# Choosing two experts of eight on GpSimd instead of VectorE in a fused attention and mixture-of-experts kernel

## The reference

```python
h = _layernorm(x) * (1 + ca) + sa
x = x + ga * attn(h)          # 16 heads of width 8, softmax, a norm over the whole sample
h = _layernorm(x) * (1 + cb) + sb
logits = h @ gate_w                                   # [token, 8]
top_vals, top_idx = jax.lax.top_k(logits, 2)          # of equals, the lower index first
gate_scores = softmax(top_vals)
x = x + gb * sum_k gate_scores[k] * expert[top_idx[k]](h)
```

## Time and profile before

| | |
|---|---|
| time, median of 3 runs | 1099.64 us (1099.56 to 1099.70) |
| profiled execution, whole | 1099.41 us |
| its span | 1097.5 us |
| mean granted PE clock over the span | 0.972 |
| busy: PE, DVE, ACT, POOL | 947.5, 922.9, 796.9, 664.2 us |
| the 1024 maxima (L1234) | 643.0 us, 680 ns each |
| the 1024 exponentials (L1773) | 544.3 us, 603 ns each |

### The profile page before, as it was taken

The page is one execution under the profiler, slowest core; times in us unless marked ns, Lnnn a source line. Parts: engine busy times, 40 slices in busy tenths (PEclk is TensorE's granted clock), DMA queues, the critical chain, the costliest instruction groups (busy, mean ns, idle before and its releaser), DMA issues. The chain is left out here.

```text
span 1097.5 us, 19321 instructions
## 1 busy us (share of the span) xinstructions
PE 947.5 (86%) x5725; PEld 360.7 (33%) x5725; DVE 922.9 (84%) x2045; ACT 796.9 (73%) x1493; POOL 664.2 (61%) x1033
## 2 busy tenths in 40 slices
PE   4699888998999999899998999888798999699970
PEld 2122222222222222222222222222125766466640
DVE  5788989999999999999999999999765677255666
ACT  2128888888888888888888888888676687477640
POOL 4843132675856768566685665634637667777772
PEclk9999999999999999999999999999879999899995
DMA  8979766856667566775656757522332454454556
GB/s 214 140 144 243 154 183 131 152 154 106 162 138 141 160 115 171 135 146 146 129 166 122 156 141 136 151 77 67 86 100 76 154 167 138 132 158 129 185 169 244
DMA packets 369047, 159.61 MB, mean 145 GB/s; under 512 B 290656, under 2 KB 333552, under 8 KB 365232
## 3 DMA queue, kind: packets, MB, share of 16 engines
q1 hardware_dynamic: 347376, 122.06, 50.3%
q10 hardware_dynamic: 12480, 17.57, 5.0%
q0 software_dynamic: 9088, 18.76, 4.9%
HBM read 87.85 MB, written 71.82 MB: 145 GB/s over the span
## 5 line engine op out<-in xcount | busy, mean ns | idle before, releaser
L1234 DVE TENSOR_REDUCE neg_max<-bank 128x1 f32<-128x512 f32 x1024 | 643.0, 680 | 34.6 <-PE bank L1998 31.8
L1773 ACT ACTIVATE probs<-bank 128x512 f32<-128x512 f32 x1024 | 544.3, 603 | 94.8 <-PE bank L2010 91.9
L1998 PE MATMUL bank<-Kt,Qt 48*128 48x512 bf16 x1024 | 339.1, 396 | 61.7 <-DVE neg_max L1234 47.3
L2010 PE MATMUL bank<-Qt,Kt 51*128 51x512 bf16 x1024 | 329.9, 390 | 6.2 <-ACT probs L1773 5.9
L2023 PE MATMUL bank<-probs,Vt 128*16 128x512 f32 x2048 | 274.2, 608 | 0.0
L1998 PEld LDWEIGHTS bank<-Kt,Qt 48*128 48x128 bf16 x1024 | 73.5, 94 | 400.6 <-DVE neg_max L1234 368.4
L1125 POOL DMA_INDIRECT y_dram<-y_rows,row_in x156 | 154.2, 988 | 56.9 <-issue 44.2
L1051 POOL DMA_INDIRECT rows_dram<-rows,slot x128 | 127.1, 993 | 45.4 <-issue 30.6
L1901 ACT ACTIVATE probs<-bank,w3b_cur 128x512 f32<-128x512 f32 x78 | 53.6, 688 | 56.2 <-PE bank L2048 56.1
L1659 DVE SCALAR_TENSOR_TENSOR probs<-bank,w3b_cur,probs 128x512 f32<-128x512 f32 x78 | 58.3, 748 | 38.4 <-ACT probs L1901 38.2
L2010 PEld LDWEIGHTS bank<-Qt,Kt 51*128 51x128 bf16 x1024 | 73.7, 93 | 35.8 <-ACT probs L1773 31.4
(11 more groups left out here) (236 smaller groups left out, 1210.4 us busy)
## 6 DMA issues: line engine op xcount, KB each, us to landing
o_dram<-o_sb ACTq DMA_DIRECT2D x64, 256.0 KB, 2.8
row_in<-rows_dram SPq DMA_DIRECT2D x39, 260.0 KB, 2.8
Qt<-q_dram SPq DMA_DIRECT2D x64, 128.0 KB
Kt<-k_dram SPq DMA_DIRECT2D x64, 128.0 KB
y_in<-y_dram SPq DMA_DIRECT2D x16, 512.0 KB, 4.8
q_dram<-q_parts SPq DMA_DIRECT2D x48, 128.0 KB, 4.9
k_dram<-k_parts SPq DMA_DIRECT2D x48, 128.0 KB, 5.6
rows_dram<-rows SPq DMA_DIRECT2D x4, 1040.0 KB, 5.5
```

The lines of the kernel that those rows point to most:

```text
L1234: dve.tensor_reduce(neg_max[:, side, a, col:col + 1], score_a[m % 3][:], AX_X, ALU.max, negate=True).then_inc(s_max, 1)
L1773: act.activation(probs[:, 4 * (j % 2) + (k ^ 1)], score_b[n % 3][:], ACT.Exp).then_inc(s_exp, 1)
L1998: pe.matmul(score_a[m % 3][:], Qt[b % BUFS][first:first + ROWS, n, P * c:P * c + P], Kt[b % BUFS][first:first + ROWS, n], start=True, stop ...
L2010: pe.matmul(score_b[m % 3][:], Kt[b % BUFS][first:first + ROWS + PARTS, n, P * c:P * c + P], Qt[b % BUFS][first:first + ROWS + PARTS, n], ...
```

## The change

In stages 3 to 16 the masks `pick` are made by POOL instead of DVE, by another method. A new function `choose(f)` runs between `gap` and `front_hits`. It subtracts the top two from the logits (`behind`) and compares with 0 (`equal`, in the upper half of a row of 16 whose lower half holds zeros). It then counts, by two shifted sums and a last one (`pairs`, `fours`, `earlier`), how many equals stand before each expert. For the second choice it takes 1 from the count where both top values are equal (`even`). A product of "count is 0" and `equal` gives `pick`. That is nine operations. DVE keeps `front_top`, with one more wait (for the pick of the block before), and loses its seven operations of quads 9 and 10 in these stages. For blocks 14 and 15 DVE chooses as before, with adjusted wait values. The diff, without the declarations of tiles and semaphores:

```diff
@@ pool
+            for m in (equal, pairs, fours):
+                pool.memset(m[:], 0.0).then_inc(s_pad, 1)
...
+            def choose(f):
+
+                pool.wait_ge(s_top, TT * (f + 1))
+                pool.tensor_tensor(behind[:], logits[:].unsqueeze(1).broadcast_to([P, 2, TT, E]),
+                                   top[:, :, 0:2].rearrange("p t k -> p k t").unsqueeze(3).broadcast_to([P, 2, TT, E]),
+                                   ALU.subtract).then_inc(s_behind, 1)
+                pool.wait_ge(s_behind, f + 1)
+                if f == 0:
+                    pool.wait_ge(s_pad, 3)
+                pool.tensor_scalar(equal[:, :, E:2 * E], behind[:].rearrange("p k t e -> p (k t) e"), 0.0, None, ALU.is_equal)                    .then_inc(s_equal, 1)
+                pool.tensor_scalar(even[:], top_gap[:], 0.0, None, ALU.is_equal).then_inc(s_even, 1)
+                pool.wait_ge(s_equal, f + 1)
+                pool.tensor_tensor(pairs[:, :, 2:2 * E], equal[:, :, 1:2 * E - 1], equal[:, :, 0:2 * E - 2], ALU.add)                    .then_inc(s_before, 1)
+                pool.wait_ge(s_before, 4 * f + 1)
+                pool.tensor_tensor(fours[:, :, 2:2 * E], pairs[:, :, 2:2 * E], pairs[:, :, 0:2 * E - 2], ALU.add)                    .then_inc(s_before, 1)
+                pool.wait_ge(s_before, 4 * f + 2)
+                pool.tensor_tensor(earlier[:], fours[:, :, E:2 * E], fours[:, :, E - 4:2 * E - 4], ALU.add).then_inc(s_before, 1)
+                pool.wait_ge(s_before, 4 * f + 3)
+                pool.wait_ge(s_even, f + 1)
+                pool.tensor_tensor(earlier[:, TT:2 * TT], earlier[:, TT:2 * TT], even[:].unsqueeze(2).broadcast_to([P, TT, E]),
+                                   ALU.subtract).then_inc(s_before, 1)
+                pool.wait_ge(s_before, 4 * f + 4)
+                pool.tensor_scalar(earlier[:], earlier[:], 0.0, None, ALU.is_equal).then_inc(s_first, 1)
+                pool.wait_ge(s_first, f + 1)
+                pool.tensor_tensor(pick[:].rearrange("p k t e -> p (k t) e"), earlier[:], equal[:, :, E:2 * E], ALU.mult)                    .then_inc(s_pick, 2)
...
                 if has(b, 3, NB):
                     gap(b - 3)
+                    pool.wait_ge(s_gap, b - 2)
+                    choose(b - 3)
                     front_hits(b - 3)
                     gap_one(b - 3)
@@ vector, front_top
                 dve.wait_ge(s_misc_full, misc_index("logits", f) + 1)
+                if f:
+                    dve.wait_ge(s_pick, 2 * f)
@@ vector, front_tied, front_best, front_pick (now blocks 14 and 15 alone)
-                if f >= NB - 2:
-                    dve.wait_ge(s_gap_exp, f)
-                    dve.tensor_tensor(top_gap[:], top[:, :, 0], top[:, :, 1], ALU.subtract).then_inc(s_gap, 1)
+                dve.wait_ge(s_gap_exp, f)
+                dve.tensor_tensor(top_gap[:], top[:, :, 0], top[:, :, 1], ALU.subtract).then_inc(s_gap, 1)
...
@@ vector, side(b, r, h)
-                    if (r, h) == (9, 1):
-                        front_tied(b - 3)
-                    if (r, h) == (9, 3):
-                        front_best(b - 3, 0)
-                    if (r, h) == (10, 1):
-                        front_pick(b - 3, 0)
-                    if (r, h) == (10, 3):
-                        front_best(b - 3, 1)
-                        front_pick(b - 3, 1)
```

More of the change, by code:

```diff
@@ L57 @@
 Y2_RING = 3
+FIRST_LAST = NB - 2
 FIRST_SUM = 4
@@ L223, in build @@
         best = sb("best", [P, 2, TT])
+        behind = sb("behind", [P, 2, TT, E])
+        equal = sb("equal", [P, 2 * TT, 2 * E])
+        pairs = sb("pairs", [P, 2 * TT, 2 * E])
+        fours = sb("fours", [P, 2 * TT, 2 * E])
+        earlier = sb("earlier", [P, 2 * TT, E])
+        even = sb("even", [P, TT])
         pick = sb("pick", [P, 2, TT, E])
@@ L400, in build @@
         s_best = sem("s_best")
+        s_pad = sem("s_pad")
+        s_behind = sem("s_behind")
+        s_equal = sem("s_equal")
+        s_before = sem("s_before")
+        s_even = sem("s_even")
+        s_first = sem("s_first")
         s_pick = sem("s_pick")
@@ L1373, in front_best @@
                 if k == 0:
-                    dve.wait_ge(s_tied, f + 1)
+                    dve.wait_ge(s_tied, f - FIRST_LAST + 1)
                     dve.tensor_tensor(coded[:], tied[:], code8[:].unsqueeze(1).unsqueeze(1).broadcast_to([P, 2, TT, E]),
                                       ALU.mult).then_inc(s_coded, 1)
-                dve.wait_ge(s_coded, 2 * f + 1 + k)
+                dve.wait_ge(s_coded, 2 * (f - FIRST_LAST) + 1 + k)
                 dve.tensor_reduce(best[:, k], coded[:, k], AX_X, ALU.max).then_inc(s_best, 1)
             def front_pick(f, k):
-                if f:
-                    dve.wait_ge(s_hits, f)
+                dve.wait_ge(s_hits, f)
                 if f == NB - 2:
                     dve.wait_ge(s_placed, f)
-                dve.wait_ge(s_best, 2 * f + 1 + k)
+                dve.wait_ge(s_best, 2 * (f - FIRST_LAST) + 1 + k)
                 dve.tensor_tensor(pick[:, k], best[:, k].unsqueeze(2).broadcast_to([P, TT, E]),
```

## The result

| | before | after |
|---|---|---|
| median | 1100.07 us (1096.70 to 1103.78, 22 runs) | 1102.93 us (1099.44 to 1105.38, 22 runs) |
| profiled execution | span 1097.5 us | span 1100.9 us |

The ratio is 1.0027, with a 95% interval of 1.0016 to 1.0038: about 3 us slower. The forecast was 1095.2 us, between 1090.5 and 1098.3. The measured time is outside the range, on the other side of no change.

The account below looks back on a forecast made before the run. DVE bounds quads 9 and 10, with ScalarE's transfer issue 0.47 us behind. 4.9 - 0.5 = 4.4 us off 1099.41 gives 1095.0, plus 0.2 for the median: 1095.2 us, range 1090.5 to 1098.3.

Parts of the forecast that it names:

- The change part by part: Prediction's account of work removed from DVE, added to GpSimd, and waits added; 4.9 - 0.5 = 4.4 us less in sum.
- The 0.91 us of idle time before `gap_exp`: ScalarE idle behind its second transfer's issue, 11.8 us over 13 stages; moves the next bound one for one.
- 0.38 a stage: Gain before the first maximum of quad 11: 0.47 - 0.09 = 0.38 us, over 13 stages 4.9 us.
- Rival 2: No change: ScalarE's second issue grows to some 1.2 us, or y_sq is held over 0.7; 1098 to 1100 us, chance 0.13.
- ScalarE's issue and not DVE is the next bound: Before quad 11's first maximum, ScalarE and TensorE allow 445.20 against DVE's 445.67: only 0.47 of 1.19 us can be gained.
- DVE's wait: DVE's wait for TensorE's first-score weight loads grows from 31.8 us by about 11 us, mostly before quad 11's first maximum.
- The nine operations: GpSimd's choice takes 2.9 us, 3.5 with handovers, inside a 5.04 us hole before hits; cost 0.
- The idle time before y_rstd: GpSimd's idle time there grows from 0.5 to about 1.2 us as hits no longer waits.
- The 0.5 us for the variance matmul: In quad 11 TensorE's variance matmul delays later score matmuls: 0.04 us over 13 stages, 0.5 us given back.
- Rival 3: Slower: GpSimd's nine operations outgrow their hole, past 7 us in all, felt at y_rstd; 1109 us at 8 us, chance 0.05.
- Rival 1: All of DVE's time comes back, 15.5 us, giving 1084 us; chance 0.10, in part as 8 to 12 us.
- The shared port: GpSimd may hold DVE's y_sq in quads 9 and 10, at most 0.43 us, covered by 0.7 us of slack.

Follow-up runs that it names:

- m3_after_last: The changed kernel with its six new tiles declared behind y_rows, so all others keep their old addresses; 1093.56 us, ratio to before 0.9956.
- m1: The kernel before plus one unused 2080-byte tile ahead of pick, giving later tiles the changed kernel's addresses; 1103.02 us, ratio to before 1.0034.
- n1: The kernel before with only q_parts and k_parts moved to 32 bytes past a multiple of 64; 1105.16 us, ratio to before 1.0047.
- m2: The changed kernel plus 32 unused bytes, so later tiles stand at multiples of 64 bytes again; 1093.59 us, ratio to before 0.9954.
- n3: m3_after_last with ScalarE's second transfer of quad 9's maxima issued after the second exponential of quad 10; 1085.55 us, ratio to before 0.9869.
- n2: The kernel before with tiles from pick on moved 32 or 96 bytes, q_parts and k_parts staying at multiples of 64; 1099.23 us, ratio to before 1.0000.
- o2: The changed kernel, store sources still off a multiple of 64, with ScalarE's second transfer issued after quad 10's second exponential; 1090.65 us, ratio 0.9916.

## Why the prediction was wrong

**The step that failed is a missing term.** "The change part by part" lists what is removed, added and waited for, and prices three memsets at the start at nothing, but it has no line for the six tiles, which are part of the change, and none for SyncE's queue, on which their effect falls. ("From quad 12 on I see nothing that the change touches" held: from quad 11 on a stage takes the same time in all kernels.) The place of `q_parts` and `k_parts` costs 1.0027 / 0.9956 = 1.0071, some 7.8 us, between the kernel after and m3_after_last, each taken against the kernel before. In the kernel before the same offset costs 3.7 (m1) to 5.2 us (n1): ratios 1.0034 and 1.0047. The difference of 2.6 to 4.1 us fits in part with ScalarE's issue, which costs more once DVE no longer stands behind it: by the traces, 13 stages lose 0.8 to 1.4 us in quads 9 and 10 with the choice on DVE (n1, m1 against before) and 2.6 to 3.5 with it on GpSimd (after against m3, m2). The intervals of the times are too wide to make sure of it.

**A second step took as fixed what moved, as a consequence of the first.** The 0.91 us of idle time before `gap_exp` was carried over from the trace of before. It rose to 16.2 / 13 = 1.25 us, and since the bound moves with it one for one, 0.38 a stage became 0.04; measured, quads 9 and 10 became 0.07 shorter in the mean. With the sources in place it stayed near its value of before (12.4 us over 13 stages in m2, 13.6 in m3, for 11.8). Rival 2 named this mechanism ("the issue of the second transfer grows to some 1.2 us in most stages") at 0.13, and priced it rightly as no change; it had no cause for it, and it could not give a loss.

**The steps that held**, read in m2 and m3, where the addresses are right. The gain is 0.9956 and 0.9954 of 1099.25: 4.8 and 5.1 us, for a forecast of 4.4; both medians, 1093.6, are within 1.7 us of 1095.2. Quads 9 and 10 became 0.34 us shorter in m2 and 0.27 in m3, for a forecast of 0.34. ScalarE's issue and not DVE is the next bound: n3 took that bound away and stages 3 to 14 went from 555.3 to 547.0 us, 0.69 each more. DVE's wait was to rise by 11 us from 31.8; it rose to 41.9 in m3 and 40.3 in m2. The nine operations were put at 2.9 us busy and 3.5 in all, and take 2.9 (0.30, 0.40, 0.21, 0.36, 0.37, 0.30, 0.24, 0.38, 0.32) and 3.4. The idle time before y_rstd was put at 1.2 us; it is 2.14: `hits` starts 4.21 us into quad 9 instead of 5.68, and y_rstd 0.2 later than before (8.30 for 8.14). The 0.5 us for the variance matmul was not tested by itself.

**Rival 3**, GpSimd outgrowing its hole, is the only one that allowed for a slower kernel, and the kernel is slower; but not for its reason. It was to begin at over 7 us for choose, choose takes 3.4, and even twice the work, 6.8 us, costs nothing that can be told. (Its 1109 us for 8 us a stage is 1095.2 + 13 = 1108 by its own numbers.) **Rival 1**, all of DVE's time, did not come out with the change alone; three quarters of the 1.19 us a stage can be had ((558.0 - 547.0) / 12 = 0.92) when ScalarE's issue is moved as well.

**The shared port.** y_sq started at 445.80, inside GpSimd's `equal` (445.72 to 446.12), and took 0.21 us: it was not held. It started inside `equal` in every stage from 3 to 13 and took 0.20 or 0.21 us each time. The Trainium skill, page "SBUF — State Buffer", section "SBUF: two separate sides", would have it blocked until the other's end, as y_sq has two SBUF inputs and `equal` reads SBUF. Here the measurement decides: for this pair no block shows. But in stage 16 of the kernel after, which has no maxima, the same operation took 0.41 us, and ended with GpSimd's `fours`, a sum of two SBUF inputs (DVE, then POOL):

```profile
816.76 0.41 DVE L1323 SCALAR_TENSOR_TENSOR y_sq<-y_dev,y_mv 128x1 f32<-128x1 f32 x1
```

```profile
816.79 0.37 POOL L944 TENSOR_TENSOR fours<-pairs 128x112 f32<-128x112 f32 x1
```

In the kernel before it took 0.21 there, with nothing running on GpSimd. So a hold of 0.2 us, as the forecast feared, does occur next to one of the nine, in the stage where it costs no maximum; in the 13 stages that were counted it was nothing. That the number of GpSimd's inputs decides is a guess from these two pairs and the cast of the earlier trace rows.

## What to carry to other kernels

A diff's declarations are part of the change: work out what each new tile does to the addresses behind it, and when a change of one engine's work comes out wrong on another's queue, try the new tiles at the end of memory or padded to a multiple of 64 bytes before doubting the change. Here the sources of stores with short runs were the ones that mattered. And when an engine is relieved and only idles, move the instruction that the next one waits behind: here the choice was worth 5 us by itself, the later issue 1, and both together 14 (1085.55 against 1099.20 us).

## What the runs showed of the hardware

- **Stores whose 64-byte runs begin 32 bytes past a multiple of 64 take longer to issue one behind the other.** Three stores of q take 2.98 us at a multiple and 3.97 off it in the stage shown, nearly all of the difference in the third, and the kernel 0.47% longer (n1), although the median time to landing of the k stores is 5.6 us in either case. Only offsets of 0 and 32 past a multiple of 64 were tried. The Trainium skill, page "DMA: Bandwidth & Descriptors", section "How a descriptor splits into AXI transactions", says that a transaction has to start at a multiple of 256 bytes and fetches unused bytes before the run, in beats of 32. By that rule, as an estimate, runs at 0, 64, 128 and 192 take 2, 4, 6 and 8 beats, and those at 32, 96, 160 and 224 take 3, 5, 7 and 9, the last in two transactions: 20% more. The direction agrees. That it is the mechanism no run here shows, nor how it gets into the issue.
- **An issue on ScalarE's queue right behind another grows with what SyncE's queue is doing; one that stands apart hardly does.** In the stage shown the second of the pair takes 0.83 us, 0.88 and 1.04 (before, n2, m3), and 1.44 with the sources off (after, n1). In stages 14 and 15, where SyncE stores no q or k, it takes 0.73 in all of them. Issued 1.5 us after the first it takes 0.73 in n3, while the stores of k are still being issued, and 0.82 in o2. Why was not tried.
- **Both kernels spread by some 3 us to either side of their median from run to run**, as much as the difference between them. The spread goes with the mean granted TensorE clock: of the 56 runs of the kernel before that stand beside the experiments, the 22 at a clock of 0.975 take 1097.8 us in the mean, the 19 at 0.972 take 1100.1. Which of the two brings the other about stays open.
